# Two-layer gated cross-attention block: rows transposed once, with the block layout of the queries made by DMA and the first keys loaded straight into block form

## What is computed

```python
qh = q.reshape(b, s, N_GROUPS, HEADS_PER_GROUP, HEAD_DIM).transpose(0, 2, 3, 1, 4)
kh = k.reshape(b, s, N_GROUPS, HEAD_DIM).transpose(0, 2, 1, 3)
scores = jnp.einsum('bghsd,bgtd->bghst', qh, kh) * scale
probs = jax.nn.softmax(scores, axis=-1)
out = jnp.einsum('bghst,bgtd->bghsd', probs, vh)
...
x = x + jnp.tanh(g_xattn[0]) * _L0_xattn_ref(_layernorm(x, axis=-1), ctx_512, ctx_512, L0_xattn_Wc, L0_xattn_bc)
x = x + jnp.tanh(g_ffn[0]) * _L0_ffn_ref(_layernorm(x, axis=-1), L0_ffn_w_gate, L0_ffn_w_up, L0_ffn_w_down)
x = x + jnp.tanh(g_xattn[1]) * _L1_xattn_ref(_layernorm(x, axis=-1), ctx_512, ctx_512)
x = x + jnp.tanh(g_ffn[1]) * _L1_ffn_ref(_layernorm(x, axis=-1), ...)
```

## Time and profile before

| | before |
|---|---|
| median of 3 runs | 654.42 us (654.09 to 656.05) |
| the profiled execution's own time | 653.18 us |
| its span, first to last instruction | 651.4 us |
| mean granted TensorE clock | 0.982 |
| PE busy | 582.7 us, 89% |
| DVE busy | 471.9 us, 72% |
| ACT busy | 436.8 us, 67% |
| POOL busy | 238.8 us, 37% |

### The profile page before, as it was taken

The page is one execution under the profiler, slowest core; times in us unless marked ns, Lnnn a source line. Parts: engine busy times, 40 slices in busy tenths (PEclk is TensorE's granted clock), DMA queues, the critical chain, the costliest instruction groups (busy, mean ns, idle before and its releaser), DMA issues.

```text
span 651.4 us, 10817 instructions
## 1 busy us (share of the span) xinstructions
PE 582.7 (89%) x3552; PEld 450.7 (69%) x3552; DVE 471.9 (72%) x1152; ACT 436.8 (67%) x812; POOL 238.8 (37%) x498
## 2 busy tenths in 40 slices
PE   0654788999999999999999999999999999999886
PEld 0332576777878777777878787777778786767675
DVE  4361878686969788796969697887969696966444
ACT  3251655677786877677777868776777778678952
POOL 5340444261534334251515343351515152341120
PEclk9975999899999999999999999999999999999999
DMA  8752007000000000000000000000000000000000
GB/s 258 217 183 75 4 17 109 18 9 18 14 21 10 22 15 18 10 18 17 17 19 15 20 9 22 14 15 12 18 9 11 8 11 10 12 7 2 10 8 17
DMA packets 24694, 21.44 MB, mean 33 GB/s; under 512 B 9872, under 2 KB 23680, under 8 KB 23744
## 3 DMA queue, kind: packets, MB, share of 16 engines
q1 hardware_dynamic: 21984, 13.04, 7.8%
q0 software_dynamic: 1888, 4.87, 2.5%
q10 hardware_dynamic: 768, 2.85, 1.5%
HBM read 12.61 MB, written 5.24 MB: 27 GB/s over the span
## 4 chain that ended last, share of the span: by engine, by line
PE 66%; ACT 13%; POOL 7%; DVE 6%; issue 5%; DMA 2%; SPq 1%; DVEq 0%; POOLq 0%; ACTq 0%
PE bank L742 12%; PE bank L750 12%; PE bank L745 12%; PE bank L789 8%; PE bank L832 7%; PE bank L744 5%; PE bank L821 4%; ACT L658 3%; POOL rt L547 3%; ACT L696 2%; ACT pt L658 2%; PE bank L818 2%; PE bank L819 2%; DMA k0a<-down_hi 2%; PE bank L911 1%
## 5 line engine op out<-in xcount | busy, mean ns | idle before, releaser
L658 ACT ACTIVATE pt<-bank 128x512 f32<-128x512 f32 x192 | 109.4, 603 | 10.1 <-PE bank L821 5.5
L1092 DVE TENSOR_REDUCE mx<-bank 128x4 f32<-128x512 f32 x128 | 86.1, 684 | 8.3 <-PE bank L789 7.4
L707 ACT ACTIVATE ht_hi<-bank 128x512 fp32r<-128x512 f32 (+1 forms) x96 | 50.4, 543 | 61.4 <-PE bank L750 60.8
L742 PE MATMUL bank<-w_r,at_hi 128*128 128x352 f32 x256 | 88.4, 346 | 3.4 <-DVE work L1200 0.9
L456 POOL TENSOR_SCALAR a_ve<-a_mv 128x1 f32<-128x1 f32 x32 | 9.1, 284 | 214.2 <-DVE a_mv L1062 213.3
L745 PE MATMUL bank<-w_r,at_lo 128*128 128x352 f32 x256 | 82.2, 323 | 0.0
L1137 DVE SCALAR_TENSOR_TENSOR work<-bank,cw,work 128x176 f32<-128x176 f32 x128 | 45.3, 395 | 42.5 <-ACT work L724 28.4
L1092 DVE TENSOR_REDUCE q0b<-bank 128x4 f32<-128x512 f32 x64 | 42.6, 688 | 42.3 <-PE bank L789 42.0
L1231 DVE TENSOR_TENSOR ht_lo<-bank,ht_hi 128x512 fp32r<-128x512 f32 (+1 forms) x96 | 58.0, 618 | 18.4 <-ACT ht_hi L707 18.4
L821 PE MATMUL bank<-qt,k 128*128 128x512 f32 x128 | 54.1, 443 | 7.4 <-DMA qt<-mt 3.3
L742 PEld LDWEIGHTS bank<-w_r,at_hi 128*128 128x128 f32 x256 | 48.4, 189 | 15.3 <-DVE work L1200 5.8
(11 more groups left out here) (163 smaller groups left out, 1540.7 us busy)
## 6 DMA issues: line engine op xcount, KB each, us to landing
w_r<-in_w POOLq DMA_DIRECT2D x1, 3168.0 KB, 13.8
x<-in_x SPq DMA_DIRECT2D x16, 128.0 KB, 2.2
work<-in_w_up ACTq DMA_DIRECT2D x2, 1024.0 KB, 9.3
k<-kd SPq DMA_DIRECT2D x128, 12.0 KB
out<-y SPq DMA_DIRECT2D x16, 128.0 KB, 1.7
w_r<-in_w POOLq DMA_DIRECT2D x1, 1536.0 KB, 7.1
kd0a<-down_hi SPq DMA_DIRECT2D x2, 512.0 KB
pt<-in_w_down SPq DMA_DIRECT2D x1, 1024.0 KB, 19.3
```

Source lines behind the costliest of these rows:

```text
L658: act.activation(pt[:, g, :], PV[g % 2][:, :], ACT.Exp, scale=float(HD[L]) ** -0.5)\
L707: act.activation(ht_hi[:, 4 * t:4 * t + cols // P, :], DOWN[b][:, 0:cols].rearrange("p (k t) -> p k t", t=P), ACT.Copy)\
L742: pe.matmul(o, a_hi, w_hi, start=first, stop=False, skip_group_check=free)
L1092: dve.tensor_reduce(o, QK[(1 + m) % 2][:, :].rearrange("p (g t) -> p g t", t=T), AX.X, ALU.max, negate=True).then_inc(S["a_r"], step)
```

## The change

The norm now writes its columns in the order (group, dimension, head in group), so that two transposes of `a_xn` give every query, transposed, with four heads side by side in each block of partitions. ACT rounds them to `qh`, DVE forms `ql` from the same bank, and SP puts `qh`, `qh` and `ql` into the three 32-partition blocks of `qt` by three DMAs of 128 KB. This holds for both layers. The keys have the matching layout in three blocks (high, low-partner, high-partner) of 96 partitions, and the rows from 96 on (`MROW`) hold the maxima and the one-hot rows. So one matmul per group gives the scores in both layers. Layer 0's first product is 8 matmuls of 256 columns in place of 4 of 512. The maxima of both layers go through one transpose, `mt` and one DMA. The first keys of units 0 and 1 are loaded into block form in `work` and rounded from there. The scratch is three copies in place of six. The upward weights are rounded in four pieces, their load is issued by SP, and the two large loads of layer 1's weights wait for them. `TIMES` has new numbers on every engine, and SP has a table now too.

```diff
-        q0a = sb("q0a", [P, HPG, G0, BLK])
-        q0b = sb("q0b", [P, HPG, G0, BLK])
-        q1 = sb("q1", [P, HPG, G1, BLK])
-        mx = sb("mx", [P, 2, 4, HPG])
+        qh = sb("qh", [P, 2, T], F32R)
+        ql = sb("ql", [P, 2, T], F32R)
+        mx = [sb(f"mx{b}", [P, G1 * HPG]) for b in range(2)]
...
+            def first_k0(s):
+                keys = ctx_t.rearrange("(u h d) (b t) -> h b d u t", u=2, h=2, t=T)
+                for h in range(2):
+                    for a in range(3):
+                        r = BLK * a + HD0 * h
+                        sp.dma_start(r0[s][r:r + HD0, h::2, :], keys[h, s]).then_inc(ld_r0[s], 16)
...
+            def attention_1(i, L):
+                yield
+                n, b = at[L, i], at[L, i] % 2
+
+                def queries(a, part):
+                    sp.dma_start(qt[b][BLK * a:BLK * (a + 1), :, :, :].bitcast(F32),
+                                 part[:, :, :].bitcast(F32)).then_inc(ld_q[b], 16)
+
+                if n >= 2:
+                    wait_part(sp, "a_s", n - 2, 8)
+                else:
+                    sp.wait_ge(S["c_zero"], 2)
+                wait(sp, "a_q_hi", n)
+                queries(0, qh)
+                queries(2, qh)
+                yield
+                wait(sp, "a_q_lo", n)
+                queries(1, ql)
...
+            def attention_2(i, L):
+                yield
+                n, b, c = at[L, i], at[L, i] % 2, i % 2
+                per = G[L] // 2
+                wait(sp, "a_mt", n)
+                sp.dma_start(qt[b][MROW:MROW + per, :, :, :].bitcast(F32),
+                             mt[0:HPG * G[L], :].bitcast(F32)).then_inc(ld_m[b], 16)
...
-                pool.tensor_tensor(q[:, :, :, d:2 * d], xv, q[:, :, :, 0:d], ALU.subtract).then_inc(S["a_q_lo"], 1)
...
-                act.activation(qt[b][:, 0, :], QK[0][:, :], ACT.Copy).then_inc(S["a_qt"], 1)
+                act.activation(qh[:, :, :], QK[0][:, 0:D].rearrange("p (u t) -> p u t", t=T), ACT.Copy)\
+                   .then_inc(S["a_q_hi"], 1)
...
+                turn(QK[0], lambda u: a_xn[:, P * u:P * (u + 1)], 2).then_inc(S["a_qt_ps"], 1)
...
+                        pe.wait_ge(ld_q[b], 48 * (n // 2 + 1))
...
-                        pe.matmul(o, k0a[c][:, g, :], qt[b][:, 0, :], start=True, stop=False)
-                        last = pe.matmul(o, k0b[c][:, g, :], qt[b][:, 1, :], start=False, stop=True)
+                    pe.matmul(o, keys[:, g, :], qt[b][:, :, 2 * g // G[L], :], start=True, stop=True).then_inc(S["a_s"], step)
...
+                dve.tensor_tensor(ql[:, :, :], QK[0][:, 0:D].rearrange("p (u t) -> p u t", t=T),
+                                  qh[:, :, :].bitcast(F32), ALU.subtract).then_inc(S["a_q_lo"], 1)
```

More of the change, by code:

```diff
@@ L41, in flamingo_block @@
     BLK = 32
+    MROW = 3 * BLK
     ROW = BLK // 2
@@ L92, in flamingo_block @@
         v0 = [sb(f"v0_{b}", [P, G0, BLK]) for b in range(2)]
-        k0a = [sb(f"k0a_{s}", [P, G0, T], F32R) for s in range(2)]
-        k0b = [sb(f"k0b_{s}", [P, G0, T], F32R) for s in range(2)]
+        k0 = [sb(f"k0_{s}", [P, G0, T], F32R) for s in range(2)]
         k1 = [sb(f"k1_{s}", [P, G1, T], F32R) for s in range(2)]
@@ L170, in flamingo_block @@
         ld_ct = [sem(f"ld_ct{b}") for b in range(2)]
+        ld_q = [sem(f"ld_q{b}") for b in range(2)]
         ld_m = [sem(f"ld_m{b}") for b in range(2)]
@@ L173, in flamingo_block @@
         ld_k0 = [sem(f"ld_k0{s}") for s in range(2)]
+        ld_r0 = [sem(f"ld_r0{s}") for s in range(2)]
+        c_first_hi = [sem(f"c_first_hi{s}") for s in range(2)]
+        c_first_lo = [sem(f"c_first_lo{s}") for s in range(2)]
         ld_k1 = [sem(f"ld_k1{s}") for s in range(2)]
@@ L292, in load_cl @@
                 sp.dma_start(cl[s][:, :], ctx_kv[i]).then_inc(ld_cl[s], 16)
-            def first_k0(i, s, hi, lo):
-                cols = slice(T * i, T * (i + 1))
-                for g in range(G0):
-                    rows = slice(HD0 * g, HD0 * (g + 1))
-                    for r in (BLK * g, BLK * g + HD0):
-                        sp.dma_start(k0a[s][r:r + HD0, g, :].bitcast(F32), hi[rows, cols]).then_inc(ld_k0[s], 16)
-                    if lo is not None:
-                        sp.dma_start(k0b[s][BLK * g:BLK * g + HD0, g, :].bitcast(F32), lo[rows, cols])\
-                            .then_inc(ld_k0[s], 16)
@@ L327, in _ @@
+            def load_k1(i, s):
+                for a in range(3):
+                    keys = kd[a].rearrange("(u h d) (b t) -> h b d u t", u=2, h=4, t=T)
+                    for h in range(4):
+                        r = BLK * a + HD1 * h
+                        sp.dma_start(k1[s][r:r + HD1, h::4, :].bitcast(F32), keys[h, i]).then_inc(ld_k1[s], 16)
+            load_x(0, 0)
+            sp.wait_ge(S["c_r0"], 1)
+            first_k0(0)
+            load_ct(0, 0)
             load_x(1, 1)
-            load_ct(0, 0)
+            sp.wait_ge(S["c_r0"], 2)
@@ L902, in ffn_1 @@
                     yield
+                    wait(pe, "f_at_hi", n)
+                    wait(pe, "f_at_lo", n)
                     c0 = 2 * E * EI
```

462 lines of the change are left out of this document (219 added, 243 removed), and 32 rows, old and new, of the table TIMES.

## The result

The changed kernel takes 676.56 us (median of 4 runs, 675.12 to 681.39), the kernel before 654.96 us beside it: a ratio of 1.033, with a 95% interval of 1.029 to 1.038. I had predicted 619 us. The profiled execution took 675.12 us, with a span of 673.2 us and a mean granted clock of 0.965.

What follows compares the result with a forecast made beforehand. PE was taken to bound the middle, chains of waits the other stages. From 653.2 us, 18.6 (middle), 12 (start), 2.7 (layer-0 units outside pairs) and 2 (end) were taken: 617.9, with 1.2 for the median 619 us, range 604 to 633.

Steps and rivals of the forecast that it cites:

- work taken from PE should count in full in the middle: Middle, 200 to 520 us: PE was taken as the bound, so its 1.95 us less work shortens each pair in full.
- the largest term: Middle: a pair goes from 35.85 to 34.3 us, and 12 pairs give 18.6 us.
- The query path: From a unit's query transposes to queries ready for PE: 3.7 to 4.1 us, covered by 3.4 us of work in layer 1.
- the forecast 0.3 us: Layer 1's first product: PE waits 0.3 us per unit for its queries, the low end of 0.3 to 0.7 us.
- The rival of late queries: Layer 1's first product waits 1.5 us or more for queries: 19 us more, 638 us; chance 0.10.
- slower than before: One wait in SP's fixed order holds every unit's queries; at 2 us per unit 683 us; chance 0.03.
- The norm's strided write: Norm on DVE: writing with a stride costs between nothing and 658 − 417 ns; taken as nothing.
- The start: Start: fewer scratch writes move unit 2's first product from 58.06 to about 46 us, 12 us gained, bounds 4 and 18.
- the bytes and not the issues fill the hole: Start: the idle hole stays because bytes, not DMA issues, fill it: 631 us; chance 0.09.
- The end: Four layer-1 units at the end save 2.4 us of PE work; 2 us counted with ACT's copies.
- layer 0's maxima are covered: Layer 0's new DMA for the maxima takes 2.4 us behind 3.2 us of PE work, so it costs nothing.
- signs of being wrong: Pair above 35 us with PE idle over 2 us, start moving under 4 us, or 256-column matmuls above 0.12 us.

Runs made afterwards that it cites:

- b4: Kernel before, order unchanged, without layer 0's second score matmul and with fewer query transposes (1.95 us less PE work a pair): 659.37 us, ratio 1.006.
- b2: Changed kernel with PE reading a constant tile for the queries of both layers, and the three query DMAs writing 128 partitions in place of 32: 654.83 us.
- a3: Changed kernel with layer 1's two large weight loads on POOL issued some 40 us later: 681.71 us, ratio 1.044.
- b1: Changed kernel with the second copy of the queries' high part issued by ACT on its own queue: 680.80 us, ratio 1.042.
- c4: Changed kernel, whole, with the drop's product on DVE right behind the comparison instead of on GpSimd: 681.70 us, ratio 1.041.
- d4: Changed kernel with attention's exponential replaced by Silu, so the weights of attention are wrong: 677.86 us, ratio 1.041.
- a1: Changed kernel with PE reading a constant tile for queries and maxima in both layers, not waiting for query DMAs, all DMAs still issued: 653.66 us, ratio 1.000.
- d1: Changed kernel with PE reading constant queries in both layers and attention's exponential replaced by Silu: 660.52 us, ratio 1.014.
- a4: Changed kernel without the second copy of the queries' high part, so the high-by-low product is missing: 655.42 us, ratio 1.003.

## Why the prediction was wrong, step by step

**The first step that failed is "work taken from PE should count in full in the middle".** It took PE's busy share for its throughput. PE was to lose 1.95 us a pair, and b4 takes that away in the old order and shortens the pair by 0.07 us. With static queries the new order is at 35.67 us, 0.18 us shorter, where the sum without its wait for queries had 34.0. The 18.6 us of the largest term shrink to about 2 us (12 × 0.18). What holds the pair goes in part through other engines: POOL's powers, the scale's and the router's together, are worth 0.41 us a pair in the kernel before, and the scale's 0.55 us with static queries and a short `drop`. Taken alone with static queries, the `drop` and the router's power are worth nothing. The rows said so in part: a matmul's duration is its latency (0.40 us for a distance of 0.23), so 314 of 320 us busy can hide short waits. PE's busy time over the whole span was 579.3 us, not the 551 us of the prediction.

**The query path was mis-sized.** Its landing was bounded at 1.8 to 2.2 us and took 3.3 us, and the whole path took 5.6 us for 3.7 to 4.1. PE's wait at L788, 2.7 us in 8 times, is the forecast 0.3 us, but by luck: the time that covers the path was mis-sized as well, 5.25 us for 3.4, and the two errors nearly cancel. The rival of late queries had the right place. Its price, 1.2 us of wait more per unit, was not needed: 0.57 us a pair at full clock, with nothing gained on the other side, is a loss. The rival "slower than before" (0.03) had the right outcome by another mechanism: SP's order doesn't hold the queries in the middle, since the first of their issues, at 351.97 us, stands right behind ACT's rounding. The 2.3 us estimated from the Trainium skill, "DMA: Bandwidth & Descriptors" (section on the anatomy of one DMA), are 1.0 us short of the landing too; for 128 partitions b2 has 2.1 us, within my rows.

The norm's strided write, taken at nothing in the sum, has a price: in the middle a layer-1 unit's `a_xn` took 0.52 us for 0.41, a layer-0 unit's 0.85 us for 0.41, and PE waits 4.4 us in 8 times for `a_xn`. Against it the feed-forward's `f_xn` fell from 0.71 to 0.51 us. No run took the stride out alone.

**The clock had no term.** In the middle it was 1.00 before, and 0.98 after. It is below 1.00 there in every profiled kernel in which layer 1's products wait for three query DMAs (after, a3, b1, c4, d4: 0.95 to 0.99) and 1.00 in all others. That costs about 6.6 us against a1, and the changed kernel's own runs spread with it, from 675.12 us at a mean clock of 0.965 to 681.39 us at 0.950. PE's idle time alone doesn't order the kernels: from 205 to 490 us it is 20.7 us in d1, at a clock of 1.00, and 17.6 us in after. I tested no kernel with the same wait and a full clock, so that the wait lowers the clock is argued, not shown.

**The start.** Predicted were 12 us for unit 2's first product, at 46 us. It came at 59.32 us, 1.3 us later than before. The kernel's very first product, left at 20 us in the prediction, came at 23.69 us, after 5.31 us of waiting for unit 0's low part. SP's queue did get shorter, as forecast: unit 2's keys were issued at 43.55 us, for 47.70 before. But unit 1's queries, on time in the queue, landed late:

```profile
33.63 0.60 SPq L369 DMA_DIRECT2D qt<-ql  x1
...
42.50 0.77 PE L784 MATMUL bank<-k,qt 96*128 96x256 f32 x2 [5.59 <-DMA qt<-ql]
...
59.32 0.63 PE L784 MATMUL bank<-k,qt 96*128 96x256 f32 x2
```

A load of 3168 KB had been issued on POOL's queue at 29.87 us, and the transfer of 128 KB took 8.7 us beside it. The rival "the bytes and not the issues fill the hole" was right for these queries: with the load moved, PE's wait for them falls from 5.59 to 0.17 us (a3), and the queries beside which the load then runs are late instead. The step that failed is that the prediction let transfers run beside each other at no cost.

It isn't the whole of the hole. In a1 PE doesn't wait for queries, and unit 2's first product still comes at 57.38 us. There PE waits for unit 1's maxima:

```profile
50.60 0.77 PE L819 MATMUL bank<-qz,k 128*128 128x512 f32 x1 [8.39 <-DMA qt<-mt]
```

Their DMA stands in SP's order behind the keys of unit 2, and SP has waited 8.6 us for the last scratch write (`kd<-down_lo`) before it issues those; in after it waits 8.0 us, in a3 3.2 us.

**The end.** I counted 2 us of gain and found 8.9 us of loss. With static queries 5.5 us of it remain (126.86 for 121.35 us), and in b4, which keeps the old order, none (121.55 us). So the new order costs something where the layer-0 units run out. In a1 PE's transposes wait 4.3 us for `a_xn` and 4.0 us for `ht_lo` from 522 us on. I didn't test which it is.

**What was right:** matmuls of 256 columns on 96 partitions cost what they did before, layer 0's L784 doesn't wait in the middle, and layer 0's maxima are covered. Two of the signs of being wrong came too: a pair above 35 us with PE idle more than 2 us in it (17.6 us in 285 us), and a start that moves by less than 4 us.

**What stays open** is the rest of the loop that holds the pair at 35.7 us. Of four links tried (the `drop`, the scale's power, the table load, the router's power) only a run with the scale's power shortened it, and the run for the table load doesn't isolate it. None of the kernels that compute all of the reference beats the kernel before.

## What to carry to other kernels

A high busy share of an engine with pipelined instructions isn't yet a bound. Before a saving on it is counted in full, take work of that size out of the kernel, with the order unchanged, and see whether the period of the loop moves. A wait shows a late partner, not the link that sets the period: shorten the partner and see what is late next. For a DMA inside the loop take a duration of the same shape at the destination, not only of the same bytes, and ask what large transfer is in flight beside it.

## What the runs showed of the hardware that I had not expected

- 128 KB from 128 partitions of SBUF into 32 partitions land 3.2 to 3.3 us after the issue (a1), into 128 partitions 2.1 us (b2).
- More of them together land later: 3.0 us with two per unit (a4), 3.2 to 3.3 us with three, and with three on two queues 2.9 us for the first and 3.7 and 3.8 us for the other two (b1). Beside a load of 3 MB on POOL's queue one took 8.7 us.
- With attention's exponential replaced by Silu, a table load of 1.28 us moved to the router's exponential (d1): what a function costs depends on what ran before it.
- POOL's power takes 0.59 us on 128x1 and 1.69 us on 128x8, a multiplication 0.21 us on either.
